# Second attention: the second keys block moved ahead of the first outputs block

## What is computed

```python
q_in = x @ Wq + _lora(x, q_down, q_up, q_alpha)
k_in = org_ctx @ Wk + _lora(org_ctx, k_down, k_up, k_alpha)   # 124 rows
v_in = org_ctx @ Wv + _lora(org_ctx, v_down, v_up, v_alpha)
out = _attention(q_in, k_in, v_in)                 # 16 heads of 64
ipa_k, ipa_v = ipa_ctx @ Wk_ipa, ipa_ctx @ Wv_ipa  # the other 4 rows
out = out + _attention(q_in, ipa_k, ipa_v)
return out @ Wo + bo + _lora(out, o_down, o_up, o_alpha)
```

## Time and profile before

| what | value |
|---|---|
| time, median of 3 runs | 526.05 us (525.59 to 528.3) |
| the profiled execution's own time | 526.27 us |
| its span | 524.5 us |
| instructions | 13371 |
| busy: TensorE matmuls, VectorE, ScalarE, GpSimd | 494.0, 396.8, 271.6, 235.3 us |
| granted TensorE clock, mean | 0.998 |

### The profile page before, as it was taken

The page is one execution under the profiler, slowest core; times in us unless marked ns, Lnnn a source line. Parts: engine busy times, 40 slices in busy tenths (PEclk is TensorE's granted clock), DMA queues, the critical chain, the costliest instruction groups (busy, mean ns, idle before and its releaser), DMA issues.

```text
span 524.5 us, 13371 instructions
## 1 busy us (share of the span) xinstructions
PE 494.0 (94%) x5109; PEld 380.1 (72%) x5113; DVE 396.8 (76%) x1064; ACT 271.6 (52%) x728; POOL 235.3 (45%) x331
## 2 busy tenths in 40 slices
PE   4799999999999998999989999999989999999996
PEld 3566666656667776777767777788757897799995
DVE  5888989766797889777897879778986678536553
ACT  3366565445666565564745575564663544513332
POOL 5845454044365542675245653533321890080540
PEclk9999999999999999999999999999999999999999
DMA  8900000000001110111000000022200300001001
GB/s 229 224 4 3 2 2 3 4 1 7 4 1 32 32 34 0 32 32 33 2 1 2 4 2 1 3 63 62 55 10 19 104 0 2 0 4 41 2 2 41
DMA packets 21872, 14.47 MB, mean 28 GB/s; under 512 B 5929, under 2 KB 21137, under 8 KB 21809
## 3 DMA queue, kind: packets, MB, share of 16 engines
q1 hardware_dynamic: 20704, 13.31, 9.7%
q10 hardware_dynamic: 1104, 0.30, 0.3%
HBM read 12.30 MB, written 1.05 MB: 25 GB/s over the span
## 4 chain that ended last, share of the span: by engine, by line
PE 74%; DVE 18%; issue 3%; ACT 2%; DMA 1%; POOL 1%; ACTq 0%; DVEq 0%; POOLq 0%
PE bank L1771 9%; PE bank L1780 5%; PE bank L1531 5%; PE bank L1443 5%; PE bank L1354 5%; PE bank L1538 4%; PE bank L1518 4%; PE bank L1700 4%; PE bank L1490 4%; PE bank L1510 4%; PE bank L1501 3%; PE bank L1787 3%; PE bank L1589 3%; PE bank L1339 3%; DVE negmax L760 2%
## 5 line engine op out<-in xcount | busy, mean ns | idle before, releaser
L498 POOL TENSOR_TENSOR work<-work,rsum 128x496 f32<-128x496 f32 x64 | 64.1, 1014 | 131.7 <-DVE rsum L778 131.7
L1130 ACT ACTIVATE work<-bank,negmax 128x124 f32<-128x124 f32 x256 | 72.5, 376 | 77.7 <-DVE ipa_s L762 77.7
L533 POOL TENSOR_SCALAR work<-work,slot 128x128 f32<-128x128 f32 x64 | 49.6, 792 | 48.3 <-DVE slot L853 29.4
L1771 PE MATMUL bank<-work 128*128 128x256 f32 x224 | 53.4, 381 | 0.0
L995 DVE SCALAR_TENSOR_TENSOR work<-work,bank 128x256 f32<-128x256 f32 x64 | 26.9, 420 | 33.0 <-ACT work L1282 32.8
L481 POOL TENSOR_TENSOR work<-work 128x512 f32<-128x512 f32 (+2 forms) x48 | 40.2, 838 | 12.1 <-DVE work L732 9.6
L1282 ACT ACTIVATE work<-bank 128x256 f32<-128x256 f32 x64 | 24.5, 383 | 40.6 <-PE bank L1771 29.1
L1771 PEld LDWEIGHTS bank<-work 128*128 128x128 f32 x224 | 40.3, 190 | 4.7 <-DVE work L998 0.2
L760 DVE TENSOR_REDUCE negmax<-bank 128x4 f32<-128x496 f32 x64 | 42.3, 661 | 0.0
L776 DVE TENSOR_REDUCE sums<-work 128x4 f32<-128x496 f32 x64 | 41.4, 647 | 0.5 <-ACT work L1130 0.5
L629 DVE TENSOR_REDUCE negmax<-bank 128x8 bf16<-128x1024 f32 x32 | 39.1, 1220 | 3.1 <-PE bank L1324 2.5
(11 more groups left out here) (197 smaller groups left out, 1082.7 us busy)
## 6 DMA issues: line engine op xcount, KB each, us to landing
work<-in_L_ffn_w_dram SPq DMA_DIRECT2D x42, 128.0 KB, 2.4
x_all<-in_x_dram SPq DMA_DIRECT2D x4, 256.0 KB, 5.3
out_dram<-x_all SPq DMA_DIRECT2D x4, 256.0 KB, 2.5
ctx_all<-in_ctx_dram SPq DMA_DIRECT2D x4, 192.0 KB, 5.8
ctx_all<-in_L_ffn_w_dram SPq DMA_DIRECT2D x6, 128.0 KB, 2.3
work<-in_L_xattn_Wq_dram SPq DMA_DIRECT2D x1, 512.0 KB, 6.8
work<-in_L_xattn_Wo_dram SPq DMA_DIRECT2D x1, 512.0 KB, 9.1
work<-in_L_ffn_We_dram SPq DMA_DIRECT2D x1, 512.0 KB, 6.6
```

The costliest lines, as they stand in the source:

```text
L498: pool.tensor_tensor(part, part, rsum1[:, b % 2, CH * n:CH * n + CH].unsqueeze(2).broadcast_to((128, CH, ORG)), ALU.mult).then_inc(Z.norm, 1)
L533: ins = pool.tensor_scalar(ohw_of(e)[:, k, :], count[:, :], slot[:, h, 0, k, e % E1:e % E1 + 1], slot[:, h, 1, k, e % E1:e % E1 + 1], ALU. ...
L1130: ins = act.activation(p1[:, b % 2, n, c, 0:ORG], blocks(bank[n])[:, c, 0:ORG], ACT.Exp, bias=negmax1[:, b % 2, CH * n + c:CH * n + c + 1])
L1771: mm = pe.matmul(halves(bank[4 + c])[:, n, :], up_weights(e, n, c), xgT[e // E1][:, :, e % E1, :], start=True, stop=True)
```

## The change

In the list of TensorE, `keys(f, 1)` stands ahead of `outputs(t, 0)` instead of between the two outputs blocks; in the list of ScalarE, its copy moves likewise, ahead of the copy of the first outputs block. The step `take(6)` of ScalarE, at b = -1 alone, where there are no outputs, moves with it. Nothing is added or removed, and what each block waits for is unchanged.

```diff
@@ ScalarE, round1 @@
                 if head_of(b):
                     head_powers(head_of(b))
+                if b == -1:
+                    take(6)
+                if there(f):
+                    act.wait_ge(Z.k1, f + 1)
+                    act.activation(k1T[:, f % 2, 4:8, 0:ORG], bank[6][:, 0:4 * ORG].rearrange("p (c n) -> p c n", c=4), ACT.Copy)\
+                        .then_inc(Z.k1_sb, 1)
                 if there(t):
                     outputs(t, 0)
                 if b == 12:
...
                 if b == B:
                     gathered(6)
-                if b == -1:
-                    take(6)
-                if there(f):
-                    act.wait_ge(Z.k1, f + 1)
-                    act.activation(k1T[:, f % 2, 4:8, 0:ORG], bank[6][:, 0:4 * ORG].rearrange("p (c n) -> p c n", c=4), ACT.Copy)\
-                        .then_inc(Z.k1_sb, 1)
@@ TensorE, round1 @@
                 if there(g):
                     pe.wait_ge(F.ys0, g + 1)
                     ffn(g, 1, bank[7])
+                if there(f):
+                    keys(f, 1, Z.k0_sb, f + 1)
                 if there(t):
                     outputs(t, 0, *p_copied(t, 2))
                 if b == 12:
...
                 if b == B:
                     gather(6)
-                if there(f):
-                    keys(f, 1, Z.k0_sb, f + 1)
```

## The result

The changed kernel takes 530.76 us (median of 10 runs, 529.96 to 533.46) against 526.87 us before (10 runs, 525.39 to 530.02): ratio 1.0074, 95% interval 1.0053 to 1.0094. It is slower by 3.9 us. I had said 527.6, within 525.3 to 529.5: the sign was right, the size was not, and the time lies outside the range.

The account below looks back on a forecast made before the run. The prediction took TensorE's list of blocks to bound the loop, with VectorE nearly full. Its terms, -0.1 + 1.42 - 0.34 + 0.61 = +1.6 us, gave 527.6 us on the median of 526.05, range 525.3 to 529.5.

Parts of the forecast that it names:

- Normal turns: Loop turns 1 to 11: 0.34 us saved on shape changes is paid back by wait and restart, -0.1 us together.
- K1's start: Second keys block in a normal turn: starts at 257.80, 0.24 us late, waiting for VectorE's copy of the first keys.
- the 0.93 and the 0.97: Normal turn on TensorE: first to second outputs block 0.93 us, second outputs block to first values block 0.97 us.
- The rival of slow block starts: Outputs blocks start slowly by themselves, both steps stay 1.02 us; +3.5 us in all, 529.5 us; chance 0.14.
- ScalarE's thin cover: First values block's wait for ScalarE's copy of the first outputs block stays hidden, with 0.1 us to spare.
- Turn 12: No expert product covers the wait, so the first values block moves from 344.53 to 345.95: +1.42 us.
- Turn 13: Router's logits keep TensorE past the copy's end, so the first values block comes at 360.69 against 361.03: -0.34 us.
- Turn 14: No product covers the wait: first values block 0.87 us later on TensorE, +0.61 us on VectorE's chain.
- absorbed: Rival: VectorE's selection work hides the losses of turns 12 and 14 on TensorE; 525.6 us; chance 0.12.
- the chance of 0.20 for slower: Whole kernel slower than 528.7 us: 0.14 from slow outputs block starts plus 0.06 upper tail of the author's sum.
- the first rival: Outputs blocks start slowly by themselves; normal turns +1.4 us for eleven, turn 13 given as -0.10; chance 0.14.

## Why the prediction was wrong

The chain of the argument held. Point by point:

- **Normal turns**, -0.1 us: measured -0.06 over ten turns, and -0.05 in the two other traces of the changed kernel. K1's start, and the 0.93 and the 0.97 as a sum, were right to 0.01 us. The rival of slow block starts is out.
- **ScalarE's thin cover** held: in turn 7 the copy of O0 runs from 261.91 to 262.51, and V0 starts at 262.67.
- **Turn 12**, +1.42: measured +1.43 where the clock stays up. **Turn 13**, -0.34: -0.35. **Turn 14**, 0.87 on TensorE and 0.61 beyond VectorE's backlog: +0.89, and +0.64 after turn 15 gives 0.25 back. None of it was absorbed; VectorE's update in turn 12 idled 3.64 us instead of 2.22.
- **The step that failed** is the price of the waits in turns 12 and 14: the sum has their length, +1.42 and +0.61, and no term for the clock. I read the granted clock of 1.00 at the start, and took it for a constant. I wrote that TensorE would stand idle for over 1 us ahead of K1 and never asked what an idle TensorE does to its clock. In two of three traces it falls behind both stretches, 3.2 us together. An estimate from these three traces, two thirds of 3.2, so 2.1, and the 1.7 make 3.8; measured were 3.9, 2.8 and 3.2 us in the three comparisons, and 3.2 over all executions together. How often a fall comes is known no better than that. The range was too narrow by this term, and so was the chance of 0.20 for slower.
- **Slips in the sum** that changed nothing: in the first rival, turn 13 should read -0.20, the 0.14 above my -0.34, and not -0.10. And the 1.67 us of VectorE ahead of turn 13's update stand in the earlier trace rows as "issue"; the update starts 0.09 us behind the projection's end at 364.91, so it follows TensorE as I said.

The Trainium skill, TensorE: Matmul & The Clock Gate, section Why this matters for your kernels, warns of idle gaps between bursts of matmuls, after which the clock goes down. The runs agree with it in kind. They differ in the size: the page has longer gaps in view than any in these turns, and the measurement decides, falls behind 1.53, 1.60 and 1.84 us. I had not gone through TensorE's idle stretches, since it is 94% busy; the two of 2.03 and 2.04 us in turns 4 and 8 of the trace of before, with the clock at 1.00, would not have warned me either, and only more traces show that the clock can fall there.

What stays open: why the kernel with the added wait, with stretches of 1.53 and 1.59 us in the same turns, had no fall in its trace and by its mean time few in its twelve executions, while the kernel moved in turns 12 and 14 had two in its trace. And why single executions differ by up to 3.4 us ahead of turn 1; falls of the clock are a part of it, as the 1.58 and 1.38 us in the seam show. At 134 to 140 us eight of the fourteen traces have a fall, and the second trace of the kernel before has one at 17 to 27 us.

## What to carry to other kernels

A reordering that saves changes of shape on a full engine can be worth nothing where the moved block must wait for another engine, as here a wait of 0.24 us and the restart behind it took back 0.34: find, at its new place, when its operand or its bank comes free, in every turn that is not like the others. Count an idle stretch on TensorE twice, once for its length and once for the chance that the clock falls behind it, here up to 1.6 us a time; where a wait can't be avoided, work put into it, even work that is thrown away, can pay. And time gained on one engine in a turn is kept only if no other engine sets the length of the next.

## What was not expected of the hardware

The clock can fall after idle stretches of 1.5 to 2.5 us on a TensorE that was busy around them: behind 4 of the eleven of 1.84 us, 6 of the ten of 1.53 to 1.60 us, 3 of the 24 of 2.03 to 2.52 us, and none of the thirteen that matmuls without use filled. Longer is not likelier in these counts, and what decides is open; in the seam it falls in eight of fourteen traces, where the longest stretch just ahead is 1.00 us. It need not fall at once: in the example above the block right behind the stretch still ran at the higher level. A fall costs 1.55 to 1.61 us in the turns that were held or changed, 1.38 in the seam, and 0.97 in turn 4, where a part of it goes into a wait for VectorE, 0.41 us at 202.07 in the trace of before, that vanishes. A mean clock of 0.98 to 0.99 over the span says nothing of where that happened; the windows by stretch do.
